# A state space layer's four-step convolution: four multiply-adds on VectorE, or four shifted products on TensorE

## The reference

```python
xz = jnp.einsum('bld,ed->ble', x, in_proj_w)           # 128 -> 512 features
x_in, z = jnp.split(xz, 2, axis=-1)                    # 256 and 256
xc = conv_general_dilated(swap(x_in), conv_w, (1,), padding=[(3, 0)],
                          feature_group_count=256)     # 4 taps over time, one filter per feature
x_in = silu(swap(xc + conv_b))
dbc = jnp.einsum('bld,ed->ble', x_in, x_proj_w)        # delta, B and C
```

## Time and profile before

| what | value |
|---|---|
| median of 3 timed executions | 3391.09 us |
| profiled execution, its own time | 3393.52 us |
| its span | 3392.3 us |
| mean granted TensorE clock | 0.82 of 2.4 GHz |
| busy: DVE, PE, ACT, POOL | 77%, 69%, 46%, 36% |
| L1338, the projection: 64 records in 8 examples | 38.5 us |
| L1347, the x projection: 64 records | 39.2 us |
| L1374, ACT copies into xpad: 16 | 9.6 us |
| L1420, DVE scaling: 16 | 7.8 us |
| L1422, first multiply-add: 8 and 8 | 6.2 and 6.2 us |

### The profile page before, as it was taken

The page is one execution under the profiler, slowest core; times in us unless marked ns, Lnnn a source line. Parts: engine busy times, 40 slices in busy tenths (PEclk is TensorE's granted clock), DMA queues, the critical chain, the costliest instruction groups (busy, mean ns, idle before and its releaser), DMA issues. The chain is left out here.

```text
span 3392.3 us, 34666 instructions
## 1 busy us (share of the span) xinstructions
PE 2336.6 (69%) x8947; PEld 1154.7 (34%) x8947; DVE 2613.5 (77%) x6691; ACT 1557.9 (46%) x3364; POOL 1210.9 (36%) x1118
## 2 busy tenths in 40 slices
PE   3068775876648786797758786487866876586854
PEld 1015222542215431363215531154313632164313
DVE  4874899779987799858898699977899588964282
ACT  2406722675226752467226652167524682263322
POOL 3020336314343153513454143341545143631471
PEclk8579787978869897797979887698878989697857
DMA  3011012131011311131110410113101311102212
GB/s 92 0 28 26 25 45 58 40 95 47 33 49 32 102 53 32 50 93 55 45 52 25 122 52 24 49 34 103 57 29 49 103 50 42 52 18 89 66 38 87
DMA packets 118905, 181.35 MB, mean 53 GB/s; under 512 B 15824, under 2 KB 55392, under 8 KB 115552
## 3 DMA queue, kind: packets, MB, share of 16 engines
q1 hardware_dynamic: 114528, 170.05, 17.9%
q0 software_dynamic: 4096, 8.40, 0.9%
HBM read 156.51 MB, written 21.89 MB: 53 GB/s over the span
## 5 line engine op out<-in xcount | busy, mean ns | idle before, releaser
L1324 POOL TENSOR_TENSOR gat<-sil,cbs 128x512 f32<-128x512 f32 x256 | 324.1, 1268 | 372.7 <-ACT sil L1289 272.1
L736 DVE TENSOR_SCALAR_CACHE_REDUCE wmask<-z,tc 128x512 bf16<-128x512 f16 x640 | 436.0, 741 | 23.4 <-ACT z L703 19.2
L1520 ACT ACTIVATE ps_rest<-cols,Aneg 128x512 f32<-128x512 f32 x256 | 175.8, 689 | 417.8 <-DVE hfc L1540 384.5
L904 POOL TENSOR_SCALAR wmask<-wmask 128x512 bf16<-128x512 bf16 x256 | 163.0, 637 | 482.4 <-DVE wmask L861 477.4
L1264 PE MATMUL ps_rest<-rest_hT,WF 128*128 128x512 f32 x512 | 291.2, 656 | 29.0 <-ACT sil L1289 28.8
L987 PE MATMUL ps_att<-z,Vp 128*32 128x128 f32 x2048 | 282.6, 285 | 20.2 <-DVE z L1059 20.2
L1254 PE MATMUL ps_rest<-gat,WP 128*128 128x512 f32 x512 | 280.0, 631 | 4.6 <-POOL gat L1324 4.3
L1289 ACT ACTIVATE sil<-ps_rest,w_b1T 128x512 f32<-128x512 f32 x256 | 174.1, 685 | 213.9 <-PE ps_rest L1264 209.0
L1037 DVE CUSTOM_DVE_ANT_0 z<-ps_att,wmask 128x512 f32<-128x512 f32 x256 | 175.6, 686 | 119.3 <-PE ps_att L975 111.9
L669 PE MATMUL ps_att<-qk 128*128 128x512 bf16 x512 | 221.7, 448 | 66.4 <-DVE g_rank L852 25.8
L1492 PE MATMUL ps_rest<-hg,ident 128*128 128x512 f32 x256 | 197.6, 864 | 98.9 <-DVE hg L1552 98.6
(11 more groups left out here) (358 smaller groups left out, 5280.2 us busy)
## 6 DMA issues: line engine op xcount, KB each, us to landing
cbs<-spreads SPq DMA_DIRECT2D x128, 256.0 KB, 3.4
WF<-in_w SPq DMA_DIRECT2D x64, 256.0 KB, 2.6
WP<-in_w SPq DMA_DIRECT2D x64, 256.0 KB, 2.6
WF<-in_wfc SPq DMA_DIRECT2D x64, 256.0 KB, 2.6
WG<-in_wgate SPq DMA_DIRECT2D x64, 256.0 KB, 2.9
WP<-in_wproj SPq DMA_DIRECT2D x64, 256.0 KB, 3.3
qk<-bounce SPq DMA_DIRECT2D x32, 384.0 KB, 6.0
bounce<-both_parts SPq DMA_DIRECT2D x72, 128.0 KB
```

Of the source, the lines that this page charges most:

```text
L736: od.up(dve.tensor_scalar(wmask[:, i, :], z_at[i], tc[:, 0, i:i + 1], None, ALU.is_ge, ALU.add, accum_out=tc[:, 1, i:i + 1]))
L1324: weighed0.up(pool.tensor_tensor(gat[m % 2], sil[m % 2], cbs[e % 2][:], ALU.mult))
L1520: decays.up(act.activation(dA[k][:], dl[:, k, :], ACT.Exp, scale=Aneg[:, k, s:s + 1]))
```

## The change

The convolution moves into the projection. A tap scales a feature's whole column of `in_projT`, so the convolved value is the sum of four products: the projection's block with its columns scaled by tap n, times the hidden state shifted by n. `rest.hT` becomes the last 512 columns of `rest.past`, which has three zero columns ahead of it, and the eight scaled 128x128 blocks are made once, at the start: PE turns the two blocks of `in_projT`, DVE makes diagonal matrices of the taps from `ident`, and PE multiplies the two, which scales and turns back at once. The first example's projection waits for these (`tapsd`). ACT reads the sums straight from PSUM, with Silu and bias in one instruction. The third and fourth block wait for banks as before, the fourth now for the first Silu. The two `xpad` tiles, ACT's two copies and DVE's eight instructions per example go. POOL clears `rest.c[2]` as soon as layer 0's result is added. The costs in the yields follow: PE 4.36 for each half, where it had 1.09.

```diff
@@ pe_late, once @@
         turnedP.up(pe.transpose(rest.bank[0][:, 0:E], wts["bproj"][:], ident[0:E, 0:E]))
+        for k in range(DC):
+            mm = pe.transpose(rest.bank[1][:, k * P:(k + 1) * P], wts["in_projT"][:, k * P:(k + 1) * P], ident[:])
+        turnedP.up(mm)
+        yield 0.8
+        yield keptI.at(0)
+        pe.wait_ge(*keptI.at(0))
+        for k in range(DC):
+            tapped.up(pe.matmul(rest.bank[2 + k][:], rest.c[0][:, k * P:(k + 1) * P], rest.c[1 + k][:], start=True, stop=True))
+        yield 2.2
@@ dve_late, once @@
+        yield 0.4
+        for k in range(DC):
+            for n in range(4):
+                od.up(dve.tensor_scalar(rest.c[1 + k][:, n * P:(n + 1) * P], ident[:], wts["m_cw"][:, k, n:n + 1], None, ALU.mult))
+        yield 2.0
+        yield turnedP.at(0, 1)
+        dve.wait_ge(*turnedP.at(0, 1))
+        od.settle()
+        keptI.up(dve.tensor_copy(rest.c[0][:, 0:DC * P], rest.bank[1][:, 0:DC * P]))
+        yield 0.5
+        for k in range(DC):
+            yield tapped.at(0, k)
+            dve.wait_ge(*tapped.at(0, k))
+            tapsd.up(dve.tensor_copy(taps[:, k].rearrange("p n c -> p (n c)"), rest.bank[2 + k][:]))
+            yield 0.7
@@ pe_mamba @@
-        for k in range(2 * DC):
+        if b == 0:
+            yield tapsd.all(0)
+            pe.wait_ge(*tapsd.all(0))
+        for k in range(DC):
+            for n in range(4):
+                mm = pe.matmul(bk[k][:], taps[:, k, n, :], rest.past[:, n:n + S], start=n == 0, stop=n == 3)
+            proj_in.up(mm)
+            yield 4.36
+        for k in range(DC, 2 * DC):
             if k >= 3:
-                yield split_in.at(b, k - 3)
-                pe.wait_ge(*split_in.at(b, k - 3))
+                yield xed.at(b, k - 3)
+                pe.wait_ge(*xed.at(b, k - 3))
             proj_in.up(pe.matmul(bk[k % 3][:], wts["in_projT"][:, k * P:(k + 1) * P], rest.hT[:], start=True, stop=True))
             yield 1.09
@@ act_mamba @@
             if k < DC:
-                split_in.up(act.activation(xpad[k][:, 3:3 + S], bk[k % 3][:], ACT.Copy))
-                yield 0.64
+                if b and k == 0:
+                    yield out1.all(b - 1)
+                    act.wait_ge(*out1.all(b - 1))
+                xed.up(act.activation(xi[:, k, :], bk[k][:], ACT.Silu, bias=wts["m_cb"][:, k:k + 1]))
+                yield 0.77
...
-        for k in range(DC):
-            yield conved.at(b, k)
-            act.wait_ge(*conved.at(b, k))
...
-            xed.up(act.activation(xi[:, k, :], c[k][1][:], ACT.Silu, bias=wts["m_cb"][:, k:k + 1]))
-            yield 0.77
@@ dve_mamba @@
-        for k in range(DC):
-            a, z = c[k]
-            yield split_in.at(b, k)
-            dve.wait_ge(*split_in.at(b, k))
-            cw = wts["m_cw"][:, k, :]
-            od.up(dve.tensor_scalar(a[:], xpad[k][:, 0:S], cw[:, 0:1], None, ALU.mult)); od.settle()
-            yield 0.52
-            od.up(dve.scalar_tensor_tensor(z[:], xpad[k][:, 1:1 + S], cw[:, 1:2], a[:], ALU.mult, ALU.add)); od.settle()
-            yield 0.99
-            od.up(dve.scalar_tensor_tensor(a[:], xpad[k][:, 2:2 + S], cw[:, 2:3], z[:], ALU.mult, ALU.add)); od.settle()
-            yield 0.79
-            conved.up(dve.scalar_tensor_tensor(z[:], xpad[k][:, 3:3 + S], cw[:, 3:4], a[:], ALU.mult, ALU.add))
-            yield 0.79
@@ pool_mamba @@
-        yield conved.at(b, DC - 1)
-        pool.wait_ge(*conved.at(b, DC - 1))
+        yield added.at(b, 0)
+        pool.wait_ge(*added.at(b, 0))
         zeroed.up(pool.memset(rest.c[2][:], 0.0))
```

More of the change, by code:

```diff
@@ L131, in emit @@
     loaded, late = sig("loaded", len(EARLY) + 1, 16), sig("late", len(LATER), 16, 30.0)
-    built, hot, cleared = sig("built", 18), sig("hot", 8), sig("cleared", 8 * FULL + 2 * E + 7)
+    built, hot, cleared = sig("built", 18), sig("hot", 8), sig("cleared", 8 * FULL + 2 * E + 6)
     siluc, modp, bop, ready = sig("siluc", 2), sig("modp", 2), sig("bop"), sig("ready", 5)
@@ L138, in emit @@
     gbh = sb("gbh", [P, B]); gbb = sb("gbb", [P, B, E])
-    wiped, turnedP, gbs = sig("wiped", 5, 16), sig("turnedP"), sig("gbs", 2)
+    wiped, turnedP, gbs = sig("wiped", 5, 16), sig("turnedP", 2), sig("gbs", 2)
+    keptI, tapped, tapsd = sig("keptI"), sig("tapped", 2), sig("tapsd", 2)
     Aneg = sb("Aneg", [P, DC, NS])
@@ L169, in emit, with __init__ @@
     class Space:
-        def __init__(self, name, norms):
+        def __init__(self, name, norms, before):
             self.nrm = sb(name + "_nrm", [P, NT, D])
@@ L175, in __init__ @@
             self.rstd = sb(name + "_rstd", [P, NT]); self.vpe = sb(name + "_vpe", [P, NT])
-            self.hT = sb(name + "_hT", [P, S])
+            self.past = sb(name + "_hT", [P, before + S])
+            self.hT = self.past[:, before:]
             self.c = [sb(f"{name}_c{i}", [P, S]) for i in range(3)]
@@ L182, in __init__ @@
             self.normed = sig(name + "_normed", norms)
-    att, rest = Space("att", 1), Space("rest", 5)
+    att, rest = Space("att", 1, 0), Space("rest", 5, 3)
     in_tiles = lambda t: t[:].rearrange("p (a b) -> p a b", b=P)
@@ L261, in emit @@
     hid = [flat(hfc2)[:, wide + u * CAP:wide + (u + 1) * CAP] for u in range(2)]
-    xpad = [sb(f"xpad{k}", [P, 3 + S]) for k in range(DC)]
+    taps = sb("taps", [P, DC, 4, P])
     xi, sz, dl, dtx = (cols[:, n] for n in range(4))
@@ L273, in emit @@
     y0, out0 = sig("y0"), sig("out0", 2)
-    proj_in, split_in, conved, xed = sig("proj_in", 4), sig("split_in", 4), sig("conved", 2), sig("xed", 2)
-    din_ps, dins, dt_ps, dts = sig("din_ps", 2), sig("dins", 2), sig("dt_ps", 2), sig("dts")
-    soft, softe, logged, stepped, y_open, zeroed = sig("soft"), sig("softe"), sig("logged"), sig("stepped"), sig("y_open"), sig("zeroed")
+    proj_in, split_in, xed = sig("proj_in", 4), sig("split_in", 2), sig("xed", 2)
+    din_ps, dins, dt_ps = sig("din_ps", 2), sig("dins", 2), sig("dt_ps", 2)
+    soft, softe, logged, stepped, zeroed = sig("soft"), sig("softe"), sig("logged"), sig("stepped"), sig("zeroed")
     keptB, outB, spreadB, spreadC = sig("keptB"), sig("outB", 1, 16), [sig(f"spreadB{i}", NS // 4, 16) for i in range(4)], sig("spreadC", NS)
@@ L361, in dve_setup @@
             cleared.up(dve.memset(base[:, :, e:e + 1], float(CAP * e - 1)))
-        for tz in (Vp, Qpad, pool_pad, xpad[0], xpad[1], rexp, cmid):
+        for tz in (Vp, Qpad, pool_pad, rest.past, rexp, cmid):
             cleared.up(dve.memset(tz[:], 0.0))
@@ L1367, in act_mamba @@
         bk = rest.bank
-        c = ((rest.c[0], rest.c[1]), (rest.c[2], cbs[0]))
         yield from act_norm(rest, b, 3, rest.bank[0], modT[1][:, b, 1:2], modT[1][:, b, 0:1], rest.hT)
@@ L1381, in act_mamba @@
                 yield 0.64
-        for k in range(DC):
-            yield conved.at(b, k)
-            act.wait_ge(*conved.at(b, k))
-            if b and k == 0:
-                yield out1.all(b - 1)
-                act.wait_ge(*out1.all(b - 1))
-            xed.up(act.activation(xi[:, k, :], c[k][1][:], ACT.Silu, bias=wts["m_cb"][:, k:k + 1]))
-            yield 0.77
         for m in range(DC):
@@ L1948, in pe_rest @@
         pe.wait_ge(*hot.all(0))
-        pe_late()
-        yield 0.2
+        yield from pe_late()
         for b in every:
@@ L1973, in dve_rest @@
         yield turnedP.at(0)
-        dve_late()
-        yield 0.4
+        yield from dve_late()
         for b in every:
```

## The result

The changed kernel takes **3443.7 us** (4 executions, 3441.3 to 3445.9) against 3392.0 (4, 3389.7 to 3396.0) for the kernel before on the same chip: 1.0149 of it, 95% interval 1.0135 to 1.0163. Forecast were 3379 and a range of 3348 to 3406. It is slower by 52 us, beyond the time of every rival.

The account below looks back on a forecast made before the run. VectorE (DVE) was taken as busiest, 77% of the span, though the layer's chain arrives last in the mamba windows. 3393.5 - 12.6 - 0.2 + 1 = 3381.7; that execution lay 2.4 above the median, so 3379 us, range 3348 to 3406.

Parts of the forecast that it names:

- What DVE gets: Mamba windows: 5.5 us of DVE freed in each, gain between 0.2 and 5.5, taken as 1.8, 12.6 us over seven.
- The cover: At the start of PE's block at most three banks stand filled with choice tiles, covering 5.0 us of DVE work.
- Rival C: Slower: choice tiles wait behind PE's long block and DVE starves, 3412 us; chance 0.23, with a bad new order.
- The chain: The layer's chain through the mamba window: 15.63 us at full clock, about 16.5 on average against 16.7, gain 0.2.
- Tiles between products: Two choice tiles per window set between PE's products, each 0.8 us gained, 1.6 us per window.
- The order: The planner lays out all queues anew from changed costs; could move the whole by 20 us either way, outside the sum.
- The block: PE's ten products before the x projection: twelve more records at 0.43 us, 8.83 us in all at full clock.
- D: Rival: shifted sources off a 16-byte border are slow on PE and wherever rest_hT is read, 3431 us; chance 0.03.
- The tail: The last example's window, running alone: gain 0.2 us, or a loss of about 3 if the clock rises late.
- The start: Making the scaled blocks once adds 4.0 us on DVE and about 2.4 on PE; cost 0 to 4, taken as 1.
- A: Rival: DVE is the bound and gains all its freed time, 38.5 us less, 3353 us; chance 0.15.

Follow-up runs that it names:

- lead 1.08: The kernel before with the planner's lead (how far the next example's attention may run ahead) at 1.08 instead of 1.12, work untouched: 1.0209 of before.

## Why the prediction was wrong

- **The step that failed is "What DVE gets".** Its term was a gain of 12.6 us, and its worst case still a gain of 0.2 per window. The work by itself cost 19 us (13 to 24). The step did count PE's time: block and x projection leave 2.2 of 16.5 us, 2.6 tiles, where DVE has 4.9 to do. It let up to three filled banks make good the rest, and so took the window's length from the layer's chain. The earlier trace rows said otherwise: PE is busy 14.4 of 16.7 us of each window already, tiles included, and 14.4 + 5.13 = 19.5 is more than the window holds. Measured: 18.3 us of PE in windows of 18.4, which were to stay at 15.5 to 17, and DVE's idle time grew by 90 us, not by some 30.
- **The cover.** In example 1 one tile covered 1.7 us of the block, not three banks 5.0. The longest wait for a tile in each of the seven windows is 6.1 to 11.4 us, and there are 9.8 us of such waits per window.
- **Rival C** had this mechanism, and its 17 us for the windows are near the work's 19. But its condition was not met: it asked for a block that starts at the half clock or exceeds 9.9 us. The block lasted 8.8 to 9.4 us in six windows, at a granted clock of 0.94 to 1.00, and 11.9 us only in the last, at 0.84. So the nearness of the two numbers is in part luck, and C's 3412 holds nothing of the order.
- **The chain.** Said was 15.63 us at the full clock and 16.5 on average, 0.2 less than before. To the end of the ACT copy it took 15.9 and 16.0 in examples 1 and 2 and 16.6 to 19.9 in the others, 17.4 on average, 0.7 more than before: choice work or a low clock came in. The windows are 1 us longer still, since DVE had tiles ahead of the cast in its queue; before, the cast followed the copy at once.
- **Tiles between products.** None stood in any of the eight; the forecast had two per window, +1.6 us gain. Forced there, they moved the loss into the chain.
- **The order.** It had ±20 and no place in the sum. It was +31 on top of the work's 19 (16 on a slower chip); lead 1.08 shows +71. Equal weight on both signs fits badly as well: every other order seen was slower.
- **Right:** DVE busy -39 (said 40). The block: 8.75 us in example 1 (said 8.83), so 0.43 per record and no penalty for shifted sources; D falls. The tail: its window is 18.37 us against 18.32. The start costs nothing (the first search begins at 70.9 us in both; I took 1). The x projection takes 3.67 to 3.70 where its records are unbroken. POOL clears at 482.62, ahead of the products. A falls: even with no products added, taking the convolution off the busiest engine gave 23 us of the 44.
- The Trainium skill, TensorE: Matmul & The Clock Gate (Back-to-back issue gap), cited with 0.216 us per 512 columns, would have made twelve records 2.6 us, so the change about 20 us cheaper; the measured 0.43 decides.

## What to carry to other kernels

Before moving work to a less busy engine, sum that engine's busy time in the very windows the work goes to: 69% over the kernel was 86% here. If that sum and the new work together are longer than the window, the window grows and the other engine waits. Price both sides by leaving the work out (42 us for the products, 23 for the convolution here) rather than by their shares. In a kernel whose queues a planner writes, run the new work in the old order before judging the work. The mirror, the old work in the new order, needs a look at where its waits stand: here they stood where they suited the other work.

## What the runs showed of the hardware

- With GpSimd's f32 TENSOR_TENSOR beside it, a VectorE SCALAR_TENSOR_TENSOR on 128x512 took 1634 ns on average (eight of eight) instead of 752, and GpSimd's own 1489 instead of 1269. The Trainium skill, SBUF — State Buffer (Who interferes with whom), says that a VectorE instruction with two inputs in this memory contends with a GpSimd one that reads it, over ports that one of them locks; the two figures agree with it.
- Chips differ by 1.1% on the same kernel: before takes 3391 us on three of them and 3429 to 3431 on two. The kernel with the first tap on ACT has a span of 3376.2 us on one and 3423.3 on another, at a granted clock of 0.82 and 0.81. 35 of the 47 us are VectorE's waits at L1037 for the attention's scores, under all releasers named. What makes these longer on some chips stays open, as does why the change's ratio is smaller there.
